# Dense convolution block with four interleaved rows per feature tile, and Vector copies for the rows between runs

## The reference

```python
def conv2d(x, w, b, pad, dil):
    y = jax.lax.conv_general_dilated(x, w, window_strides=(1, 1), padding=[(pad, pad), (pad, pad)],
                                     rhs_dilation=(dil, dil), dimension_numbers=('NCHW', 'OIHW', 'NCHW'))
    return y + b[None, :, None, None]
x1 = jax.nn.relu(conv2d(x, w1, b1, 2, 2))
x2 = jax.nn.relu(conv2d(jnp.concatenate((x, x1), 1), w2, b2, 2, 2))
x3 = jax.nn.relu(conv2d(jnp.concatenate((x, x1, x2), 1), w3, b3, 2, 2))
x4 = jax.nn.relu(conv2d(jnp.concatenate((x, x1, x2, x3), 1), w4, b4, 2, 2))
fea = jax.nn.relu(jnp.concatenate((x, x1, x2, x3, x4), 1))
fea = jnp.einsum('ij,bcjk,lk->bcil', H, fea, H)
out = conv2d(fea, w6, b6, 1, 1) + x
...
out = jax.nn.relu(_qconv(x, w1))
out = jax.nn.relu(_qconv(out, w2, stride=1, padding=1, groups=PLANES))
out = _qconv(out, w3)
return out + x
```

## Time and profile before

| | |
|---|---|
| median of 3 runs | 414.45 us (412.85 to 415.64) |
| the profiled execution: its time and its span | 414.64 us, 412.9 us |
| PE, PEld busy | 376.5 us (91%), 271.5 us (66%) |
| DVE busy | 297.1 us (72%) |
| ACT busy | 233.8 us (57%) |
| D<-D transfers (halos) | 96 of 126 KB, 2.3 us to landing |

### The profile page before, as it was taken

The page is one execution under the profiler, slowest core; times in us unless marked ns, Lnnn a source line. Parts: engine busy times, 40 slices in busy tenths (PEclk is TensorE's granted clock), DMA queues, the critical chain, the costliest instruction groups (busy, mean ns, idle before and its releaser), DMA issues. The chain is left out here.

```text
span 412.9 us, 8055 instructions
## 1 busy us (share of the span) xinstructions
PE 376.5 (91%) x2878; PEld 271.5 (66%) x2881; DVE 297.1 (72%) x545; ACT 233.8 (57%) x377; POOL 16.8 (4%) x17
## 2 busy tenths in 40 slices
PE   8699679899999999899999999999987598899986
PEld 7477558576878778686877788686765243355532
DVE  5675656958784795678489748846886599767886
ACT  4333835643765475457537664842675599078761
POOL 6000000900000000000000000000000000000000
PEclk9899999999999999999999999999999599999999
DMA  7636235233513453243336224133400000000004
GB/s 240 190 103 171 49 79 116 95 88 77 138 55 70 105 143 88 51 103 97 88 83 163 63 63 107 44 89 77 102 0 3 0 1 0 2 2 3 2 16 187
DMA packets 19533, 32.56 MB, mean 79 GB/s; under 512 B 4528, under 2 KB 11568, under 8 KB 19504
## 3 DMA queue, kind: packets, MB, share of 16 engines
q1 hardware_dynamic: 19504, 32.17, 29.8%
HBM read 11.38 MB, written 2.10 MB: 33 GB/s over the span
## 5 line engine op out<-in xcount | busy, mean ns | idle before, releaser
L705 PE MATMUL sums_ps<-D,w_hl 128*128 128x512 f32 x504 | 123.5, 399 | 6.1 <-DMA D<-D 4.3
L705 PEld LDWEIGHTS sums_ps<-D,w_hl 128*128 128x128 f32 x504 | 93.5, 188 | 37.4 <-DMA D<-D 9.4
L796 PE MATMUL mix_ps<-mix_hl,F_hl 128*128 128x288 f32 x360 | 65.2, 298 | 5.9 <-ACT Y L357 1.4
L357 ACT ACTIVATE Y<-mix_ps 128x288 f32<-128x288 f32 x120 | 48.5, 410 | 31.8 <-PE mix_ps L800 20.1
L796 PEld LDWEIGHTS mix_ps<-mix_hl,F_hl 128*128 128x128 f32 x360 | 55.0, 190 | 10.5 <-issue 5.3
L314 ACT ACTIVATE r<-sums_ps,bias_sb 64x512 f32<-64x512 f32 x28 | 19.0, 682 | 43.5 <-PE sums_ps L705 43.3
L441 DVE CAST D<-r 64x512 fp32r<-64x512 f32 x48 | 19.9, 414 | 27.0 <-ACT r L314 21.4
L450 DVE TENSOR_TENSOR r<-mix_ps,r 64x512 f32<-64x512 f32 x16 | 11.1, 693 | 37.3 <-ACT r L322 37.1
L800 PE MATMUL mix_ps<-mix_hl,X 96*128 96x288 f32 x120 | 35.3, 298 | 0.0
L1001 ACT ACTIVATE q_I<-ps,w_bias 128x1024 f32 x24 | 25.4, 1110 | 16.6 <-PE ps L1232 16.6
L443 DVE TENSOR_TENSOR D<-r,D 64x512 fp32r<-64x512 f32 x48 | 32.9, 685 | 1.6
(11 more groups left out here) (134 smaller groups left out, 507.1 us busy)
## 6 DMA issues: line engine op xcount, KB each, us to landing
D<-D SPq DMA_DIRECT2D x96, 126.0 KB, 2.3
F<-r SPq DMA_DIRECT2D x96, 64.0 KB, 2.0
x_own<-in_x_pads SPq DMA_DIRECT2D x16, 288.0 KB, 3.9
F<-in_x_mix SPq DMA_DIRECT2D x16, 128.0 KB, 2.7
xb<-in_x_res SPq DMA_DIRECT2D x8, 256.0 KB, 2.8
out<-q_res SPq DMA_DIRECT2D x8, 256.0 KB, 2.0
w_raw<-in_w_conv SPq DMA_DIRECT2D x6, 192.0 KB, 4.5
w_raw<-in_w_int SPq DMA_DIRECT2D x1, 843.0 KB, 4.6
```

Of the source, the lines that this page charges most:

```text
L357: nc.scalar.activation(Y[:, u, g], banks(p, u)[:, g % 4, 0:MIX], ACT.Copy).then_inc(y_out, 1)
L705: last = nc.tensor.matmul(conv_sums(s, u)[:, bank, :], w_hl[:, wp, n, d, :], D[f][u][:, xp, :, 4 * d:4 * d + RUN], start=start and d == 0 ...
L796: nc.tensor.matmul(y, F_hl[u][:, xp, h, k], mix_hl[:, wp], start=n == 0, stop=False, skip_group_check=True)
```

## The change

Four image rows, in place of two, are interleaved in each tile row. `ROWS` goes from 8 to 4 and the run from 64 to 128 elements, with 8 zeros on each side, so D keeps its size and a matmul reads four runs. A tile row a now holds rows 4a, 4a + 1 of the upper half of the image and 4(a + 4), 4(a + 4) + 1 of the lower half. A shift by one tile row therefore goes right for all but one: the lower half's first row needs the upper half's last one, and the reverse. SP's `halos` copies three tile rows in place of seven eighths (432 elements of 576 in place of 504), and Vector's new `edges` fills in what wraps: two copies of 32 partitions x 2 parts x 32 columns x 2 rows for each feature and image. TensorE waits for `edge_in` beside `halo_in`.

```diff
-ROWS = 8
-RUN = 2 * S
-PITCH = RUN + 8
+ROWS = 4
+SIDE = 4
+EDGE = 2 * SIDE
+RUN = SIDE * S
+PITCH = RUN + 2 * EDGE
...
 def by_rows(pixels):
-    return pixels.rearrange("p (a l b) -> p a b l", l=S, b=2)
+    return pixels.rearrange("p (a l b) -> p a b l", l=S, b=SIDE)
...
             def own(f, u, h):
-                return D[f][u][0:64, h, :, 4:4 + RUN].rearrange("p a (l b) -> p a b l", b=2)
+                return D[f][u][0:64, h, :, EDGE:EDGE + RUN].rearrange("p a (l b) -> p a b l", b=SIDE)
...
+            def edges(s, f, u):
+
+                dve.wait_ge(own_ready[u], s * 3 + f)
+
+                def side(block, row, first):
+                    return D[f][u][block:block + 32, :, row, EDGE:EDGE + RUN]\
+                        .rearrange("p h (l b) -> p h l b", b=SIDE)[:, :, :, first:first + 2]
+
+                nc.vector.tensor_copy(side(HALO_M2, 0, 2), side(OWN_T2, ROWS - 1, 0).bitcast(F32))
+                nc.vector.tensor_copy(side(HALO_P4, ROWS - 1, 0), side(OWN_T, 0, 2).bitcast(F32))\
+                    .then_inc(edge_in[f][u], 1)
...
-                    nc.vector.memset(d[0:64, :, :, 0:4], 0.0)
-                    nc.vector.memset(d[0:64, :, :, PITCH - 4:PITCH], 0.0)
+                    nc.vector.memset(d[0:64, :, :, 0:EDGE], 0.0)
+                    nc.vector.memset(d[0:64, :, :, PITCH - EDGE:PITCH], 0.0)
                     nc.vector.memset(flat[HALO_M2:HALO_M2 + 32, :, 0:HALO], 0.0)
                     nc.vector.memset(flat[HALO_P4:HALO_P4 + 32, :, DSZ - HALO:DSZ], 0.0).then_inc(zeroed, 1)
...
                     turn_s1(p - 1, 0)
                     turn_s1(p - 1, 1)
+                edges(s, 1, 0)
                 split(s, 1, 1)
+                edges(s, 1, 1)
...
                 split(s, 2, 1)
+                edges(s, 2, 0)
+                edges(s, 2, 1)
...
                 split(s, 3, 0)
+                edges(s, 3, 0)
                 split(s, 3, 1)
+                edges(s, 3, 1)
...
                         last = nc.tensor.matmul(conv_sums(s, u)[:, bank, :], w_hl[:, wp, n, d, :],
-                                                D[f][u][:, xp, :, 4 * d:4 * d + RUN],
+                                                D[f][u][:, xp, :, EDGE * d:EDGE * d + RUN],
...
             def conv2(s, u):
                 pe.wait_ge(halo_in[2][u], (s + 1) * 32)
+                pe.wait_ge(edge_in[2][u], s + 1)
```

More of the change, by code:

```diff
@@ L106, in dense_block @@
         D = [[sb(f"D{f}{u}", [NP, 2, ROWS, PITCH], F32R) for u in range(2)] for f in range(4)]
-        r = [sb(f"r{u}", [64, 8, 2, S]) for u in range(2)]
+        r = [sb(f"r{u}", [64, ROWS, SIDE, S]) for u in range(2)]
         F = [sb(f"F{u}", [NP, 2, HALF]) for u in range(2)]
@@ L130, in dense_block @@
         halo_in = {f: [sem(f"halo_in{f}{u}") for u in range(2)] for f in range(1, 4)}
+        edge_in = {f: [sem(f"edge_in{f}{u}") for u in range(2)] for f in range(1, 4)}
         conv0_done, conv_done = [[sem(f"{n}{u}") for u in range(2)] for n in ("conv0_done", "conv_done")]
@@ L748, in conv_alone @@
                 for d in range(3):
-                    last = nc.tensor.matmul(bank, w_hl[:, 0, n, d, :], D[f - 1][u][:, 1, :, 4 * d:4 * d + RUN],
+                    last = nc.tensor.matmul(bank, w_hl[:, 0, n, d, :], D[f - 1][u][:, 1, :, EDGE * d:EDGE * d + RUN],
                                             start=False, stop=d == 2, skip_group_check=True)
@@ L752, in conv_alone @@
                 for d in range(3):
-                    last = nc.tensor.matmul(side, w_hl[:, 1, n, d, :], D[f - 1][u][:, 0, :, 4 * d:4 * d + RUN],
+                    last = nc.tensor.matmul(side, w_hl[:, 1, n, d, :], D[f - 1][u][:, 0, :, EDGE * d:EDGE * d + RUN],
                                             start=d == 0, stop=d == 2, skip_group_check=True)
@@ L758, in conv1_alone @@
                 pe.wait_ge(halo_in[1][u], (s + 1) * 32)
+                pe.wait_ge(edge_in[1][u], s + 1)
                 if not is_first(s):
@@ L773, in conv3 @@
                 pe.wait_ge(halo_in[3][u], (s + 1) * 32)
+                pe.wait_ge(edge_in[3][u], s + 1)
                 conv_alone(s, u, 4, 5)
@@ L1356, in lay_out @@
                             w_conv[q, :, n, :, h, j, :] = w[:, :, u - j + 1, :].transpose(1, 2, 0)
-    x_pads = np.zeros((B, 4, C, ROWS, 2, S + 4), np.float32)
+    x_pads = np.zeros((B, 4, C, ROWS, SIDE, S + 4), np.float32)
     for q, u in enumerate((0, 2, -2, 4)):
-        for a, b in np.ndindex(8, 2):
-            if 0 <= 4 * a + b + u < S:
-                x_pads[:, q, :, a, b, 2:2 + S] = f["x"][:, :, 4 * a + b + u]
+        for half, a, b in np.ndindex(2, ROWS, 2):
+            row = 4 * (ROWS * half + a) + b + u
+            if 0 <= row < S:
+                x_pads[:, q, :, a, 2 * half + b, 2:2 + S] = f["x"][:, :, row]
     x_pads = x_pads.transpose(0, 1, 2, 3, 5, 4)
@@ L1369, in lay_out @@
     w_mix[0:96, 1] = np.tile(w6[4], (3, 1))
-    x_mix = f["x"].reshape(B, C, 8, 2, 2, S).transpose(0, 1, 3, 2, 4, 5)
+    x_mix = f["x"].reshape(B, C, 2, ROWS, 2, 2, S).transpose(0, 1, 4, 3, 2, 5, 6)
     H = f["L0_conv_H"]
@@ L1379, in lay_out @@
     h_cols[:] = h_rows.transpose(1, 0, 2)[:, :, order]
-    j = np.arange(S).reshape(8, 2, 2).transpose(1, 0, 2).reshape(S)
+    j = np.arange(S).reshape(2, ROWS, 2, 2).transpose(2, 1, 0, 3).reshape(S)
     h_rows = h_rows[:, j].reshape(3, S, PH, 2).transpose(0, 1, 3, 2)
```

## The result

The changed kernel takes 441.24 us (median of 5 runs, 439.09 to 442.13), the kernel before 414.6 us beside it: 1.063 times as long, 95% interval 1.060 to 1.067. The forecast was 417.6 us, at most 422.

The account below looks back on a forecast made before the run. The bound was taken as a chain of latencies, the ring, with Vector's stretch longest. 414.64 us plus 0.95 (start) and 3.1 (ring), less 0.8 (halos) and 0.26 (matmuls), gave 417.6 us; range 414.5 to 422.

Parts of the forecast that it names:

- Strides of 16 bytes: Split's accesses to D and reads of sums in PSUM at step 4, not 2: priced at nothing, 0.8 ns per element at most.
- stride rival: D's new step slows splits, four of six on the ring: 19.5 us at most, 437 us, half price 427; chance 0.17.
- the ring: Dense block's step as a closed chain of waits, twice through Vector, with some 12 of 96 matmuls; change adds 3.1 us.
- edge copies: Two Vector copies per feature and image, 218 ns each, 0.49 us a pair with gaps; 0.45 us a step, 3.1 in all.
- The new wait of `conv2`: Feature 2's copies for image 0 end just when its halo lands, so conv2's added wait costs nothing or a tenth.
- The halos: Transfers of 108 KB for 126 land 0.087 us sooner; nine to eleven on the ring gain 0.8 us, bounds 0 and 1.0.
- The start: Zeroing twice as long pads, eight memsets of 0.12 us more before the first split: 0.95 us lost, bounds 0.8 and 1.1.
- The matmuls: Four breaks between runs fewer, 2 ns per matmul, some 130 on the ring: 0.26 us gained, bounds 0 and 2.2.
- their rival: TensorE itself is the bound, all 768 convolution matmuls count, breaks cause a 17 ns loss: 407 us, or 401; chance 0.06.
- Edits at no cost: Names, row order in x_pads, x_mix and the transforms' matrices are the host's; later stages read the same sizes: nothing.
- a chain of latencies: The claimed limit in the dense block, Vector's 9 us stretch its longest part; other matmuls run beside the ring.
- The four waits: TensorE's waits in the sixth pair's step: 0.8 us for add_second, 0.8 for the transposes, 0.6 twice for a halo transfer.

Follow-up runs that it names:

- experiment 1: A program of its own: single Vector, ScalarE and GpSimd operations on 64 x 512 elements, read or written at steps of 1 to 16 elements; 137.99 us in all.
- experiment 6: Kernel before, 16 of 48 splits (feature 1 image 1, feature 3 image 0) writing at 16-byte steps, pads zeroed 8 wide: 416.25 us, ratio 1.004; all 48 so: 1.041.
- experiment 7: Changed kernel with the 96 edge copies moved from Vector to GpSimd, nothing left out: 434.22 us, ratio 1.044 to the kernel before.
- experiment 8: Kernel before, each convolution matmul reading 512 adjacent elements in one run in place of eight runs of 64: 413.92 us, ratio 0.999.
- Experiment 9: Kernel before, Vector's low_f of image 1 moved behind convolution 4's adds: 412.73 us, ratio 0.996; second kernel, ScalarE's high_f(1) also later, adds before low_4(0): 410.34 us, 0.990.
- experiment 11: Changed kernel with the ScalarE and Vector orders of the second kernel of Experiment 9, nothing left out: 434.99 us, ratio 1.047 to the kernel before.
- unit_stride: Changed kernel with split reading and writing adjacent elements in place of every fourth, edge copies kept: 419.45 us, ratio 1.009 to the kernel before.

## Why the prediction was wrong

**The step that failed** is "Strides of 16 bytes", where I took nothing. The price measured is 0.62 us a split. The row I kept as the other end, 0.8 ns per element from L582, was the right size: 0.406 us over 512 elements is 0.79 ns for the subtraction (0.41 forecast at most), 0.42 ns for the CAST (0.4 forecast at most). I set it aside because that row also writes 128 results and L551 one, and because PSUM is read at large steps at no loss. The second is true (the add of L453 keeps its 693 ns at the new step) and was no argument: SBUF and PSUM differ here. The case of a rival whose price has one row and whose denial has none asked for more than 0.17, or for a range up to 437. The rule that SBUF wants two hits on each line of 16 bytes (the Trainium skill, "SBUF — State Buffer", "Door 1: The DMA port swizzle") held for 4-byte elements on Vector: 8 bytes free, 16 not (experiment 1). For 2-byte elements it did not (last section).

**The stride rival's place was right, its sum was short.** Four splits of six lie on the ring, as that rival had it: 2.47 us in the sixth pair's step against 2.48, less in the steps that were longer before (experiment 6). Its 437 us is 417.6, with the edge copies in it, and 19.5 for the strides, and the time is 441. The strides alone cost less than that, 4.0% or 16.8 us. What no sum of mine had is that the two costs meet at one wait. By the unrounded ratios they cost 4.04 and 0.94% alone and 6.31% together, 1.3% more than the sum. In the sixth pair's step the copies cost 1.11 us behind strided splits and 0.53 alone, and 0.43 of these 0.58 us is cover that the splits had used up (0.89 us of wait for 1.32). Seven such steps are 4.1 us by my estimate, 1.0%; the intervals of the ratios, up to half a percent to each side, don't tell that from 1.3%.

**What held.** *The edge copies:* 220 ns each for 218; alone they cost 0.53 us a step where I had 0.45. Ratio 1.009 is 3.9 us, for the 3.0 of my sum. *The ring:* Vector's two waits were nearly the copies' whole cover, and the waits for `add_second` and the transposes grew. *The new wait of `conv2`:* I gave it nothing or a tenth; it is 1.45 us in the step shown, and costs nothing all the same (experiment 7). *The halos:* 2.2 us. *The start:* the first split begins at 12.37, 0.81 us later, for 0.95. *The matmuls:* 2.2 ns each for 2; the 17 ns that their rival built on fell with experiment 8. *Edits at no cost:* none showed.

**What was only half right.** I called the limit a chain of latencies, and the other matmuls room beside it. Experiment 9 shows the room is 0.6 us of a step of 36.57. The four waits that I read as TensorE's are PEld's, of weight loads beside running matmuls. Of the matmuls themselves the same view, 189 to 227 us, has one wait:

```profile
PE mix_ps L796 <- DVE Zt L492: 0.3, 1, 0.3
```

The busy share of 36.13 in 36.60 had said so: ring and TensorE are nearly as long as each other, so what lengthens the ring soon costs its full price (2.47 of 2.48 us in the sixth pair's step), and what shortens it gives little.

## What to carry to other kernels

Before you change a layout for TensorE, cost each operation of the other engines that reads or writes it at its new step: for 4-byte elements in SBUF one alone in 16 bytes costs Vector 0.4 to 0.8 ns more per element, while neighbours in pairs are free. Two costs behind one wait share its cover, so price them together, in the order in which they use it up. Where a row gives a price and nothing in the trace gives its absence, the range must reach to that price. And read a wait of the weight loads beside the matmuls' own: only the second is time that TensorE loses.

## What I had not expected of the hardware

The first three are from experiment 1, 512 elements, mean ns of one.

ScalarE pays as Vector does; L101 and L103 write with a step of 1 and 4, L107 reads with a step of 4 (a written step of 2 takes 661 ns):

```profile
L101 ACT ACTIVATE wc<-rc 64x512 f32<-64x512 f32 x3 | 1.9, 629 | 9.1 <-DVE rc L57 9.0
...
L103 ACT ACTIVATE wc<-rc 64x512 f32<-64x512 f32 x3 | 3.4, 1117 | 0.1
L107 ACT ACTIVATE wc<-rc 64x512 f32<-64x512 f32 x3 | 3.3, 1109 | 0.1
```

GpSimd too: 606 ns adjacent, 637 at a step of 2, 1078 at a step of 4. For 2-byte elements the price is higher, and a step of 8 bytes, free for 4-byte ones, is not; L91 to L93 subtract bf16 and write with steps of 1, 4 and 8 elements:

```profile
L91 DVE TENSOR_TENSOR ha<-hb 64x512 bf16<-64x512 bf16 x3 | 1.3, 417 | 0.1
L92 DVE TENSOR_TENSOR ha<-hb 64x512 bf16<-64x512 bf16 x3 | 3.9, 1285 | 0.1
L93 DVE TENSOR_TENSOR ha<-hb 64x512 bf16<-64x512 bf16 x3 | 7.2, 2413 | 0.1
```

A step of 8 bytes has two hits on each line of 16, so the rule named above would call it free. A lone element of 2 bytes in 8 or 16 costs 1.7 and 3.9 ns more than adjacent ones. The adjacent case is itself faster than that of 4-byte elements (417 ns for 684), and losing this could be part of it; but against 684 ns there are still 1.2 and 3.4 ns. Why is open; no kernel here has such a write.

With the reorder of experiment 11 TensorE's second wait in `conv2` grew to 1.86 and 2.01 us in two steps of the profiled execution, and both times the lower granted clock came behind it and took over 1 us. In a step of the changed kernel with waits of 1.42 and 1.33 us at the same places the clock stayed at 1.00. But the length of a wait doesn't settle it: behind 2.59 us of wait, at 83.12 us in the changed kernel, the 36 matmuls of `conv0` took 8.57 us at a clock of 1.00, and behind 2.03 us in `unit_stride` 10.13 us at 0.83 on the mean. What decides is open.
